# First mixture-of-experts block: first layer as three fp16 part products, three bias buffers, stacks cleared ahead of the scatter, two experts' weights split at the start

## What is computed

```python
scores = (tanh(xf @ gate_w.T) + 1.0) * 0.5            # xf: 2048 tokens, 8 experts
vals, idx = top_k(scores.T, 256)                      # every expert takes 256 tokens
y = layernorm(xf[idx], ln_gamma, ln_beta)             # 256 tokens of an expert, 256 features
h = gelu(einsum('knd,nfd->knf', y, fc1s) + b1s)       # first layer, 256 -> 1024
o = einsum('knf,ndf->knd', h, fc2s) + b2s             # second layer, 1024 -> 256
out = xf.at[idx].add(o * vals)                        # weighted, added back to the tokens
```

## Time and profile before

| | |
|---|---|
| median of 3 runs | 1168.98 us (1166.55 to 1169.14) |
| the profiled execution, its own time | 1166.72 us |
| its span in the profile | 1165.0 us |
| mean granted clock of TensorE | 0.963 |
| busy over the span | PE 91%, DVE 66%, ACT 58%, POOL 46% |
| busy from 601.0 to 615.3 us (one round of an expert) | PE all of it, ACT 3.35 us, DVE 1.92, POOL 10.02 |

### The profile page before, as it was taken

One profiled execution on the slowest core, in us unless ns is written; L12 is line 12 of the kernel. 1 busy time (PEld: TensorE's weight loads), 2 busy tenths in 40 slices (PEclk: granted clock), 3 DMA queues, 4 the chain that ended last, 5 costly groups with the idle time before them and its releaser, 6 DMA issues. The chain is left out here.

```text
span 1165.0 us, 28797 instructions
## 1 busy us (share of the span) xinstructions
PE 1055.8 (91%) x10263; PEld 770.9 (66%) x10264; DVE 771.1 (66%) x2213; ACT 679.0 (58%) x1286; POOL 530.4 (46%) x599
## 2 busy tenths in 40 slices
PE   6999999999999999984799998598998866999996
PEld 3666777766776677673388885344454445888885
DVE  5888887898789987968501115667777774555553
ACT  5888876777768876757332226367667653343331
POOL 4677544464455433301336640566667523233312
PEclk9999999999999999995799999899999977999998
DMA  7633433333234433307736536514444241111110
GB/s 257 163 80 85 91 74 74 92 83 72 49 83 92 83 73 74 74 11 237 247 127 182 181 64 212 169 57 120 138 128 141 63 136 37 29 28 30 27 15 10
DMA packets 120028, 116.17 MB, mean 100 GB/s; under 512 B 43488, under 2 KB 100064, under 8 KB 119776
## 3 DMA queue, kind: packets, MB, share of 16 engines
q1 hardware_dynamic: 112608, 105.27, 32.0%
q0 software_dynamic: 7296, 9.25, 4.6%
HBM read 59.89 MB, written 21.82 MB: 70 GB/s over the span
## 5 line engine op out<-in xcount | busy, mean ns | idle before, releaser
L637 ACT ACTIVATE e<-masked,neg_max 128x512 f32<-128x512 f32 x256 | 184.4, 720 | 56.7 <-DVE neg_max L763 52.9
L737 DVE TENSOR_TENSOR e_t_lo<-et,e_t_hi 128x512 f16<-128x512 f32 x256 | 176.3, 689 | 39.9 <-ACT e_t_hi L630 38.1
L763 DVE CUSTOM_DVE_ANT_0 masked<-sc,mask_bias 128x512 f32<-128x512 f32 x256 | 175.2, 685 | 23.6 <-issue 21.6
L630 ACT ACTIVATE e_t_hi<-et 128x512 f16<-128x512 f32 x256 | 150.8, 589 | 59.0 <-PE et L510 58.0
L510 PEld LDWEIGHTS et<-ident,e 128*128 128x128 f32 x1024 | 123.2, 140 | 62.3 <-issue 15.1
L510 PE MATMUL et<-ident,e 128*128 128x128 f32 x1024 | 154.9, 274 | 2.3 <-ACT e L637 0.8
L2181 ACT ACTIVATE d_e<-d_st 128x384 f32<-128x384 f32 (+1 forms) x192 | 94.0, 526 | 48.5 <-PE d_st L2324 43.8
L73 PE MATMUL ob<-v_hi,e_t_hi 128*128 128x65 f16 x1024 | 119.0, 193 | 1.2 <-issue 1.2
L74 PE MATMUL ob<-v_lo,e_t_hi 128*128 128x65 f16 x1024 | 119.2, 193 | 0.0
L75 PE MATMUL ob<-v_hi,e_t_lo 128*128 128x65 f16 x1024 | 118.4, 193 | 0.0
L73 PE MATMUL h_hb<-h_xt_hi,experts_hi 128*128 128x256 f16 x352 | 96.6, 274 | 3.8 <-DVE h_xt_lo L2555 3.8
(11 more groups left out here) (486 smaller groups left out, 2761.3 us busy)
## 6 DMA issues: line engine op xcount, KB each, us to landing
kk<-nat_k SPq DMA_DIRECT2D x64, 256.0 KB, 3.5
raw<-in_fc SPq DMA_DIRECT2D x16, 1024.0 KB, 7.5
qq<-nat_q SPq DMA_DIRECT2D x64, 128.0 KB, 2.6
qk<-scratch_stack SPq DMA_DIRECT2D x64, 128.0 KB
scratch_stack<-kq_hi SPq DMA_DIRECT2D x16, 256.0 KB, 3.3
scratch_stack<-kq_lo SPq DMA_DIRECT2D x16, 256.0 KB, 3.5
d_expert_raw<-in_gate_w SPq DMA_DIRECT2D x8, 512.0 KB, 3.9
d_expert_raw<-in_up_w SPq DMA_DIRECT2D x8, 512.0 KB, 3.6
```

The costliest lines, as they stand in the source:

```text
L630: nc.scalar.activation(e_t[u % NBUF].hi[:], et[u % 2][:], ACT.Copy).then_inc(turned_hi, 1)
L637: nc.scalar.activation(e[u % NBUF][:], masked[u % NBUF][:], ACT.Exp, bias=neg_max[:, g % 2, j:j + 1], scale=-1.0).then_inc(exp_ok, 1)
L737: nc.vector.tensor_tensor(e_t[u % NBUF].lo[:], et[u % 2][:], e_t[u % NBUF].hi[:], ALU.subtract).then_inc(turned_lo, 1)
L763: nc.vector.tensor_tensor_reduce(masked[u % NBUF][:], sc[j % 2][:], mask_bias[g // PAIRS % 2][:, j % QT, :], -SCALE0, 3e38, ALU.add, ALU.m ...
```

## The change

- **First layer.** `first_layer` calls `three_products` on fp16 parts of the weights (`fc1_parts`, two buffers, in the listings `fc_0_hi`, `fc_0_lo`, `fc_1_hi`, `fc_1_lo`) and of the scaled tokens (`yt_parts`). It waits for the low parts of both (`yt_lo`, `fc1_lo`). 16 fp32 matmuls an expert become 48 fp16 matmuls of 256 columns.
- **Parts.** ACT makes the high parts: `turned_high(e)` (one instruction of 128x512) and `weights_high(e)` (two of 128x1024). DVE makes the low parts: `turned_low(e)` (128x512) and `weights_low(e)` (two of 128x1024). Experts 0 and 1 are split at the start of the stage, ahead of the keys. In round `e` ACT does the gelus of `e`, then `turned_high(e + 1)`, then `weights_high(e + 2)`; DVE does `scale_turned(e + 1)`, `turned_low(e + 1)`, `weights_low(e + 2)`, then `weigh(e - 1)`.
- **Loads.** `load1(e)` waits for the low part of expert `e - 2` (`fc1_lo`) instead of that expert's first layer. Its place on SP's stream stays.
- **POOL.** `wb2` has three buffers, and `clear_stacks` and `fill_constants` stand ahead of the scatter.

```diff
-        wb2 = [sb(f"wb2_{i}", [P, HALVES, D]) for i in range(2)]
+        wb2 = [sb(f"wb2_{i}", [P, HALVES, D]) for i in range(WB0)]      (WB0 = 3)
@@ sync
                 for e in range(2, E):
-                    sp.wait_ge(h_full, GR * (e - 1))
+                    sp.wait_ge(fc1_lo, DT * (e - 1))
                     W.load1(sp, dram, e)
                     sp.wait_ge(fc2_done, HALVES * (e - 1))
                     W.load2(sp, dram, e)
@@ gpsimd
-                    if e >= 2:
-                        pool.wait_ge(res_ok, HALVES * (e - 1))
+                    if e >= WB0:
+                        pool.wait_ge(res_ok, HALVES * (e - WB0 + 1))
...
-                    if e >= 1:
-                        scatter(e - 1, range(HALVES))
                     if 1 <= e <= QBUF:
                         clear_stacks(e - 1)
                     if e == QBUF + 1:
                         fill_constants()
+                    if e >= 1:
+                        scatter(e - 1, range(HALVES))
@@ scalar
+                def turned_high(e):
+                    act.wait_ge(affine, e + 1)
+                    if e >= 2:
+                        act.wait_ge(h_full, GR * (e - 1))
+                    nc.scalar.activation(yt_parts[e % 2].hi[:], yt[e % 2][:], ACT.Copy).then_inc(yt_hi, 1)
+
+                def weights_high(e):
+                    act.wait_ge(W.fc1_in[e % 2], 16 * (e // 2 + 1))
+                    if e >= 2:
+                        act.wait_ge(h_full, GR * (e - 1))
+                    for c in range(DT):
+                        nc.scalar.activation(fc1_parts[e % 2].hi[:, c, :], W.fc1[e % 2][:, c, :], ACT.Copy).then_inc(fc1_hi, 1)
+
+                weights_high(0)
+                weights_high(1)
...
+                turned_high(0)
                 for e in range(E):
...
+                    if e + 1 < E:
+                        turned_high(e + 1)
+                    if e + 2 < E:
+                        weights_high(e + 2)
@@ vector
+                def turned_low(e):
+                    dve.wait_ge(yt_hi, e + 1)
+                    nc.vector.tensor_tensor(yt_parts[e % 2].lo[:], yt[e % 2][:], yt_parts[e % 2].hi[:], ALU.subtract).then_inc(yt_lo, 1)
+
+                def weights_low(e):
+                    for c in range(DT):
+                        dve.wait_ge(fc1_hi, DT * e + c + 1)
+                        nc.vector.tensor_tensor(fc1_parts[e % 2].lo[:, c, :], W.fc1[e % 2][:, c, :], fc1_parts[e % 2].hi[:, c, :], ALU.subtract).then_inc(fc1_lo, 1)
+
+                weights_low(0)
+                weights_low(1)
...
                 scale_turned(0)
+                turned_low(0)
                 for e in range(E):
                     if e + 1 < E:
                         scale_turned(e + 1)
+                        turned_low(e + 1)
+                    if e + 2 < E:
+                        weights_low(e + 2)
                     if e >= 1:
                         weigh(e - 1)
@@ tensor
-                    pe.wait_ge(W.fc1_in[e % 2], 16 * (e // 2 + 1))
-                    pe.wait_ge(affine, e + 1)
+                    pe.wait_ge(yt_lo, e + 1)
+                    pe.wait_ge(fc1_lo, DT * (e + 1))
...
-                                mm = pe.matmul(hb[n % 2][:, i, :], W.fc1[e % 2][:, c, f * P:(f + 1) * P], yt[e % 2][:, c, :], start=(c == 0), stop=(c == DT - 1))
+                                cols = slice(f * P, (f + 1) * P)
+                                mm = three_products(pe, hb[n % 2][:, i, :], (fc1_parts[e % 2].hi[:, c, cols], fc1_parts[e % 2].lo[:, c, cols]),
+                                                    (yt_parts[e % 2].hi[:, c, :], yt_parts[e % 2].lo[:, c, :]), c == 0, c == DT - 1)
```

More of the change, by code:

```diff
@@ L1448, in phase_experts0 @@
         sb, ps = make_tensors(nc, ctx)
+        WB0 = 3
         yg = [sb(f"yg{i}", [P, HALVES, ROW0]) for i in range(2)]
         yt = [sb(f"yt{i}", [P, DT, CAP]) for i in range(2)]
+        yt_parts, fc1_parts = [Split(sb, f"yt{i}", [P, DT, CAP]) for i in range(2)], [Split(sb, f"fc1_{i}", [P, DT, FF0]) for i in range(2)]
         h = [sb(f"h{i}", [P, FT0, CAP]) for i in range(2)]
-        wb2 = [sb(f"wb2_{i}", [P, HALVES, D]) for i in range(2)]
+        wb2 = [sb(f"wb2_{i}", [P, HALVES, D]) for i in range(WB0)]
         res = [sb(f"res{i}", [P, HALVES, D]) for i in range(2)]
@@ L1460, in phase_experts0 @@
         keys_full, consts = sem("fkeys_full"), sem("fconsts")
+        yt_hi, yt_lo, fc1_hi, fc1_lo = (sem("f" + n) for n in ("yt_hi", "yt_lo", "fc1_hi", "fc1_lo"))
         gathered = [sem(f"fgathered{i}") for i in range(2)]
@@ L1495, in weigh_bias @@
                     pool.tensor_copy(T.slot_weight[:, e, :], yg[e % 2][:, :, D + e]).then_inc(weight_ok, 1)
-                    if e >= 2:
-                        pool.wait_ge(res_ok, HALVES * (e - 1))
+                    if e >= WB0:
+                        pool.wait_ge(res_ok, HALVES * (e - WB0 + 1))
                     pool.wait_ge(weight_ok, e + 1)
                     for n in range(HALVES):
-                        op = pool.tensor_scalar(wb2[e % 2][:, n, :], W.bias2[:, e, :], T.slot_weight[:, e, n:n + 1], None, ALU.mult)
+                        op = pool.tensor_scalar(wb2[e % WB0][:, n, :], W.bias2[:, e, :], T.slot_weight[:, e, n:n + 1], None, ALU.mult)
                     op.then_inc(wb2_ok, 1)
@@ L1581, in weigh @@
                         nc.vector.scalar_tensor_tensor(out=res[e % 2][:, n, :], in0=ob[e % 2][n], scalar=T.slot_weight[:, e, n:n + 1],
-                                                            in1=wb2[e % 2][:, n, :], op0=ALU.mult, op1=ALU.add).then_inc(res_ok, 1)
+                                                            in1=wb2[e % WB0][:, n, :], op0=ALU.mult, op1=ALU.add).then_inc(res_ok, 1)
+                def turned_low(e):
[7 more added lines that the diff above has]
+                weights_low(1)
                 for n in range(KEYS_ROUTE, KEYS_FIRST):
```

## The result

| | before | changed |
|---|---|---|
| median | 1169.06 us (1166.55 to 1170.59, 4 runs) | 1210.83 us (1205.78 to 1212.26, 4 runs) |
| ratio of the two | | 1.0355, 95% interval 1.0332 to 1.0377 |
| the profiled execution, its own time | 1166.72 us | 1212.26 us |
| its span | 1165.0 us | 1210.5 us |
| mean granted clock | 0.963 | 0.938 |

The change made the kernel 41.8 us slower, against a prediction of 1211 (42.8 us above the kernel before) in a range of 1197 to 1221. That the median lies within 0.2 us of 1211 is in part luck: its four executions lie between 1205.78 and 1212.26, and the two profiled executions differ by 45.5 us.

A forecast was written before the change was run, and what follows sets the result against it. PE's work bounds the experts' stage. Five passes lengthened by the load wait and clock add 43.2 us, the start 1.3, pass 7 takes off 1.7: +42.8 us, forecast 1211 us, range 1197 to 1221.

The forecast's parts named there:

- The wait that the change adds: Passes 2 to 6: gelus stand behind ACT's split, which waits for load1; a pass 20.76 us at full clock.
- landing after the issue: Passes 2 to 6: load1 lands 7.7 us after SP issues it, at 8.31 us into the pass.
- two high parts: ACT in passes 2 to 6: splitting the weights after the load lands takes 2.10 us, until 10.41 us.
- PE goes on: Passes 2 to 6: PE resumes with groups 2 and 3 after the first group's two gelus, at 11.25 us.
- PE's pause: Passes 2 to 6: PE stands still from 3.05 to 11.25 us, 8.2 us, waiting for the first gelu.
- two groups: First layer, passes 2 to 6: groups 2 and 3 are 24 products, 2.61 us at full clock.
- The clock: Passes 2 to 6: the pause brings half clock to the work behind it, 2.1 us more a pass.
- the rival of a held clock: Passes 2 to 6: same waits but no clock fall, 10.5 us less, 1200.5 us; chance 10%.
- a clock that stays down through the second layer: Passes 2 to 6: half speed through second layer too, 9.5 us lost a pass, 1248 us; chance 4%.
- The start: Start of the experts' stage: early splits delay the keys; pass 2 begins at 602.4, not 601.10, +1.3 us.
- DVE and POOL: Passes 2 to 6: DVE's low parts and weighing, and POOL's buffers, clearing, scatters and gathers, cost nothing.
- The faster rival: ACT's stream, passes 2 to 6: weights landed before the split, so gelus are not held; 1160 us, chance 3%.

The follow-up runs named there:

- the wait alone: Kernel before with plain copies for 62 transposing transfers, plus ACT waiting for load1(e + 2) behind expert e's gelus and reading one column, no splits: 1211.86 us, ratio 1.0378.

## Why the prediction was right

The mechanism was the one named, the order on ACT, and the terms of a pass came out close. The agreement to 0.2 us is closer than the sum deserves: it rests on errors of a few tenths that cancel, on a start that came out right by other parts than predicted, and on where the medians fell.

**The wait that the change adds.** Shown: by the four lines of waits, and by the run of the wait alone, which has the same loss without any of the rest. Term by term, from the start of a pass:

| term | predicted | changed kernel, passes 2 to 6 |
|---|---|---|
| load1 issued | 0.61 | 0.61 (pass 3) |
| landing after the issue | 7.7 | 7.6 (7.5 to 7.7) |
| two high parts | 2.10 | 2.00 |
| PE goes on | 11.25 | 10.89 to 11.09 |
| PE's pause | 8.2 | 7.67 to 7.86 |
| two groups | 2.61 | 2.61 at the full clock |
| clock | 2.1 | 1.46 to 2.9, mean 2.39 |
| pass | 22.9 | 22.90 |

The landing and the splits were a little shorter, the clock took 0.3 us more, and the two cancel. PE's pause also began a little later than predicted, at 3.22 us and not 3.05 in pass 3. The gelus of the two waiting groups also ran faster than I counted: four in 1.55 us, so 0.77 for a pair instead of 0.84.

**The clock.** I had one 8 us pause to go by and left open whether five would all be followed by half speed. They are, in the rows of all five passes (mean clocks of 0.78 to 0.84), and so are the 5.0 to 6.1 us pauses of the wait alone. The Trainium skill, "TensorE: Matmul & The Clock Gate", section "HAM oscillation — how this bites in real kernels", tells of a loop whose short bursts of matmuls are followed by waits for transfers, and in which every round starts again at the reduced clock. The traces agree as far as the work behind a wait goes, five times out of five at 0.50. The rounds here are not short bursts (PE is busy for 14.2 to 15.6 us of each), and the first 3 us of every pass still ran at the full clock. So the rival of a held clock (1200.5) fell. The one of a clock that stays down through the second layer (1248) fell too: most of the second layer ran at the full clock, 6.9 to 7.3 us long. What the clock took was worked out from the rows (time from PE's going on to the second layer, less 2.61, and what the second layer was over 6.90). No kernel was run in which the clock is held, so that this time would come back in full is inferred.

**The start.** The third block of keys moved as said. Timeline of the changed kernel:

```profile
570.57 3.90 ACT L1563 ACTIVATE fc_hi<-raw 128x1024 f16<-128x1024 f32 x4 [2.39 <-PEq L1020]
...
571.66 4.63 DVE L1614 TENSOR_TENSOR fc_lo<-raw,fc_hi 128x1024 f16<-128x1024 f32 x4 [1.61 <-ACT fc_hi L1563]
...
576.20 1.40 DVE L1620 SCALAR_TENSOR_TENSOR kq_lo<-f_kb,bqk,kq_hi 128x512 f16<-128x512 f32 x2
577.01 0.39 PE L73 MATMUL f_kb<-ctx_t_hi,w_hi 128*128 128x512 f16 x1 [1.41 <-DVE kq_lo L1620]
...
582.40 0.39 PE L73 MATMUL f_hb<-yt_hi,fc_hi 128*128 128x256 f16 x1 [0.89 <-DVE yt_lo L1609]
...
591.59 0.28 PE L73 MATMUL f_hb<-yt_hi,fc_hi 128*128 128x256 f16 x1 [0.71 <-DVE yt_lo L1609]
```

The stage itself began 1.2 us later in this execution (570.59 against 569.36). With that taken off, the third block of keys begins at 575.8 (predicted 576.1), the first layer of expert 0 at 581.2 (581.5) and pass 2 at 602.5 (602.4). So the start cost 1.4 us, where the prediction said 1.3. This is luck in part. The prediction's own terms, 2.6 - 2 x 1.68 + 1.7, add up to 0.9 and not to 1.3, and they came out otherwise. Expert 0's first layer began 2.3 us later, not 2.6. Its round, up to the next transposes, took 7.82 us in place of 8.01, so it gave back 0.2 us where 1.68 were counted: the clock was at 0.50 from 582 to 585 us and those transposes waited 0.94 us for gathered tokens. Pass 1 gave back 0.7 us (13.52 in place of 14.25), with a wait of 0.71 us for the tokens' low part where 1.7 were counted.

The gathered tokens came late for a reason that the prediction did not have. Two of POOL's instructions that issue the gathers took twice as long while DVE made its four low parts (571.66 to 576.29). First the changed kernel, then the one before:

```profile
572.86 2.01 POOL L1493 DMA_INDIRECT yg<-scratch_y,slot_token  x1 [0.31 <-issue]
575.17 1.94 POOL L1493 DMA_INDIRECT yg<-scratch_y,slot_token  x1 [0.30 <-issue]
...
571.63 0.98 POOL L1490 DMA_INDIRECT yg<-scratch_y,slot_token  x1 [0.30 <-issue]
572.91 0.95 POOL L1490 DMA_INDIRECT yg<-scratch_y,slot_token  x1 [0.30 <-issue]
```

With the stage's later start taken off, the fourth gather was issued 2.0 us later than before (577.42 against 574.16). The run of the wait alone, which has no low parts, shows 0.98 and 0.95 us there. That DVE's work is what slows them was not tested by a run of its own.

**DVE and POOL.** Cost nothing, as said. The weighing ended 11.6 + 0.9 = 12.5 us into pass 3 (638.24 on), against 12.6 predicted and the second layer at 16.1. POOL's scatter then waited for it 9 times, 77.9 us in all, and no transpose waited for the gathered tokens longer than 1.9 us, both of those in the start. Whether three bias buffers and the earlier clearing are worth anything in a pass that is not held up was not tried.

**The faster rival** needed a landing within 1.2 us; the shortest of the five was 7.5. It said how much PE would gain if ACT were not held up, 8.8 us below the kernel before. That stays an estimate: the two ways that I see to reach it (issue the first-layer load of expert e + 1 ahead of the second-layer load of expert e, or split the weights of e + 1, not e + 2, behind the gelus of e) were not run. So it is not shown that the products win anything once the wait is gone. The first layer of pass 7, 5.23 us, shows only that the products reach their pace where nothing holds them.

## What to carry to other kernels

An engine with 10 us idle in 14 can still set the time: what counts is which of its instructions waits for what, and what is queued behind it. Before work is added to an in-order engine, follow its wait to the issue of the transfer that it needs, and see behind which wait that issue stands; here the added work on ACT was 2 us in front of the gelus and a pass grew by 8.7 us, and with the same wait and next to no work it grew by 7.7. A pause in the matmuls then costs more than its length, since the work behind it begins at half the clock: 2.4 us for each pause of under 8 us here.

## What I had not expected

A short pause was enough for the clock; the prediction had allowed for that at the start only, as up to 2 us of its range. In the run of the wait alone PE paused for only 2.1 us in pass 1, and the clock fell after work had begun again:

```profile
593.18 1.22 PE L1623 MATMUL f_hb<-yt,raw 128*128 128x256 f32 x3 [2.11 <-ACT h L1562]
...
590.00:592.00 2.00, 1.06 (x5) 0.58 (x4) 0.00 (x0) 0.00 (x0) 0.00 (x0) 1.00 0.77 311
592.00:593.00 1.00, 0.00 (x0) 0.00 (x0) 0.00 (x0) 0.81 (x3) 0.00 (x0) 1.00 0.00 0
593.00:594.00 1.00, 0.82 (x3) 0.73 (x4) 0.00 (x0) 0.85 (x3) 0.00 (x0) 0.83 0.00 0
594.00:596.00 2.00, 2.00 (x6) 1.56 (x6) 0.00 (x0) 0.00 (x0) 0.00 (x0) 0.50 0.00 0
596.00:598.00 2.00, 2.00 (x9) 1.68 (x8) 0.00 (x0) 0.84 (x2) 0.00 (x0) 0.73 0.00 0
```

The two groups behind it took from 593.18 to 598.42, 5.24 us in place of 3.45, so a pause of 2.1 us cost 3.9. The start of the changed kernel has the same: pauses of 1.4, 1.9 and 0.9 us between 575 and 582.4 us, and the clock at about 0.50 from 582 to 585 us. In the kernel before, pauses of 1.6 and 0.8 us at the same place were not followed by a fall. What separates the two I can't say from these runs. And the price of a pause varies between passes of the same kernel, from 1.46 to 2.9 us in the change and from 1.6 to 3.2 with the wait alone, as the clock came back sooner or later after work had begun.
